# Row sums of every second transposed tile: folded on VectorE and multiplied once, instead of multiplied slice by slice

## The chip, the core and the metric

The kernel runs on one core of a Trainium2 chip. The core has TensorE (matrix products into PSUM banks of 128 x 512), VectorE and ScalarE (elementwise work and reductions), GpSimd and SyncE (here mostly queues that issue transfers), and 16 DMA engines that they share. Each engine runs its own instructions in program order and waits for the others by semaphores. The metric is device time in microseconds (us) for one execution.

## What is computed

Two layers of a graph network on 8192 nodes with 128 features. Cut to what matters:

```
adj_hat = adj + I
d = 1 / sqrt(sum(adj_hat, axis=1))
h = relu((adj_hat * d[:, None] * d[None, :]) @ (x @ W) + b)     # layer 0
x = layernorm(x + h)
s = x @ weight
o = relu(s + adj @ s + x @ self_weight)                           # layer 1
x = layernorm(x + pair_norm(o))
```

adj is 8192 x 8192 in f32, 268 MB, and is read about twice. The scale d needs the sum of each row of adj before any product of layer 0 with that row's z = d * (x W) can begin.

## The kernel before, in words

**Tiling.** adj is cut into 8 x 8 blocks of 1024 x 1024. A block comes as four chunks (q = 0..3) of 1 MB, each of two slices (JB = 2) of 128 x 1024. A chunk is loaded transposed (adjT) when it is multiplied and untransposed (adjN) when only its row sums are taken. Raw chunks go through a ring of buffers: four of their own (raw0 to raw3) and, for a time, parts of s1 and zr that are not in use yet (s34, s56, z67, z45, z23). SyncE's queue issues all these loads in one order; a load waits until the chunk that had its buffer is used up (`chunk.freed`).

**Products.** Matrix products are made in the rounded format f32r. ScalarE copies a slice rounded into hi (L514), VectorE subtracts to get the rest, lo (L687), and TensorE multiplies hi and lo with the rounded and hi with the rest of z: six products of 512 columns a slice (L982, L984, L988). hi and lo are rings of four slices (DEEP = 4): ScalarE may write slice n when TensorE has finished slice n - 4 (semaphore slice_multiplied), VectorE follows ScalarE (hi_ready), TensorE follows VectorE (slice_split).

**Stages.** Layer 0 starts before all row sums are known. In stage k (1 to 7) column k - 1 is multiplied: first its diagonal block (kept in o1, no load), then the blocks of rows k to 7, one after the other, four chunks each. The row sums of row i over columns left of the diagonal come from these same transposed slices: `add_sums` (L964) multiplies the slice's hi and lo with a pick matrix that has ones in one column, so that the sum lands in row i of the banks pC and pD: four more products a slice. The sums over columns right of the diagonal of row k are made from untransposed chunks that are loaded beside the products of stage k: on ScalarE as a copy with an accumulator (L520), for q = 3 on VectorE as a reduction (L693). The diagonal block of row k is loaded into o1 beside them ("keep"), and VectorE adds its eight slices into colsum by seven additions of 128 x 1024 (`sum_kept`, L703 and L707), each of which waits for the one before.

**The end of a stage.** After the eighth chunk from a stage's end (tail 0) TensorE runs `close_sums` (L998: two full-precision products of pick with colsum), ScalarE copies pC and pD (`read_sums`), TensorE turns them (`turn_degree`, L1008, tail 2), VectorE makes the degree (tail 4), TensorE `first_product` (L1018, tail 4), VectorE `make_z` (L736 to L741, tail 6). `add_visit_up` (L750) adds a finished row's products into ux, one chunk later. Which of these stand where is written by hand into the loops over the chunks, one loop an engine.

The table that follows the chunks sets which unit sums what (`Chunk.act`), whether a product chunk carries row sums (`Chunk.summed`), and when its buffer is free.

Of the kernel before, what the change touches and what calls it, by code (L numbers as in the profile page):

```python
# [8 lines left out]
class Chunk:  # L9
# [7 lines left out]
    cached: bool = False  # L17
    act: bool = False
    summed: bool = False
    stage: int = -1  # L20
    tail: int = -1
    buf: str = ""
# [29 lines left out]
def graph_kernel(nc, x, xT, adjT, adjN, W0, b_rows, W1, Wself, out):  # L52
    f32 = mybir.dt.float32
# [5 lines left out]
    P = 128  # L59
# [3 lines left out]
    BLK = 1024  # L63
    NB = N // BLK
    assert NB == 8
    Q = 4
    JB = 2
    TILE = JB * BLK
    HALF = 512
    H = 2  # L70
# [14 lines left out]
    def multiply_block(into, row, col, layers, visit, **more):  # L85
        for q in range(Q):
            into.append(Chunk("mul", row, col, q, layers=layers, visit=visit, **more))

    def new_visit(row, layers, phase, **more):
        visits.append(Visit(row, layers, phase, **more))  # L90
        return len(visits) - 1

    TAIL = 2 * Q
    products = []
    beside = defaultdict(list)
    for k in range(NB):
        sums = []
        for c in range(k + 1, NB):
            for q in range(Q):
                sums.append(Chunk("sum", k, c, q, act=(q % 2 == 0 if k == 0 else q != 3), stage=k))  # L100
        kept = [Chunk("keep", k, k, q, stage=k) for q in range(Q)]
        if k == 0:
            chunks += kept + sums
            continue
        first = len(products)
        multiply_block(products, k - 1, k - 1, (L0,), new_visit(k - 1, (L0,), 1, first=(k == 1)),
                       cached=True, stage=k)
        for i in range(k, NB):
            multiply_block(products, i, k - 1, (L0,), new_visit(i, (L0,), 1, first=(k == 1)),
                           summed=True, stage=k)  # L110
        for i, c in EXTRA.get(k, ()):
            multiply_block(products, i, c, (L0,), new_visit(i, (L0,), 1), stage=k)
        for n in range(first, len(products)):
            products[n].tail = n - (len(products) - TAIL)


        at = max(2 * Q, min(3 * Q, len(sums)))
        if k >= NB - 2:
            sums += [None] * (at - len(sums))
        sums[at:at] = kept  # L120
        room = [1.0] * Q + [0.5 if k < NB - 2 else 1.0] * Q + [1.0] * (len(products) - TAIL - first - Q)
        share, put = len(sums) / sum(room), 0
        if k >= NB - 2:
            share = 1.0
        for n in range(len(room)):
            upto = round(share * sum(room[:n + 1]))
            beside[first - Q + n] += [c for c in sums[put:upto] if c]
            put = max(put, upto)
        assert put >= len(sums)
# [39 lines left out]
    after_row0 = next(c for c in chunks if c.stage == 1)  # L169


    slices = act_sums = dve_sums = 0
    for chunk in chunks:
        if chunk.kind == "mul":
            chunk.base = slices
            slices += JB
            chunk.freed = ("split", slices)
            visits[chunk.visit].end = slices
        elif chunk.kind == "sum" and chunk.act:
            act_sums += 1  # L180
            chunk.freed = ("act", act_sums)
        elif chunk.kind == "sum":
            dve_sums += 1
            chunk.freed = ("dve", dve_sums)
# [106 lines left out]
    with ctx:  # L291
# [6 lines left out]
        def sem(name):  # L298
            return ctx.enter_context(nc.semaphore(name))
# [29 lines left out]

        xT_blk = s1[:, 0:BLK]  # L330
        colsum = s1[:, BLK:2 * BLK]
        rsum = [s1[:, 2 * BLK + r * NB * BG:2 * BLK + (r + 1) * NB * BG] for r in range(2)]
        kept = o1
        raw = {f"raw{r}": raw_own[r][:, :] for r in range(4)}
# [17 lines left out]
        sums = [pC, pD]  # L352
# [11 lines left out]
        act_summed = sem("act_summed")  # L364
        dve_summed = sem("dve_summed")
        col_step = sem("col_step")
        sums_closed = sem("sums_closed")
        sums_read = sem("sums_read")
        deg_turned = sem("deg_turned")
# [38 lines left out]
        dve_normed = sem("dve_normed")  # L408
        out_done = sem("out_done")

        raw_free = {"split": slice_split, "act": act_summed, "dve": dve_summed}
        bank_free = {"row": row_summed, "l0": l0_read, "dual": dual_read, "added": dual_added, "l1": l1_read,
                     "x1": x1_ready, "s1": s1_ready, "self": self_added}

# [14 lines left out]
        def slice_of(chunk, j):  # L429
            if chunk.kind == "keep" or chunk.cached:  # L430
                return kept[:, chunk.q * TILE + j * BLK:chunk.q * TILE + (j + 1) * BLK]
            return raw[chunk.buf][:, j * BLK:(j + 1) * BLK]
# [16 lines left out]
        @block.gpsimd  # L449
        def _(pool):  # L450
            pool.dma_start(w0[:, :], W0).then_inc(consts_in, 16)
            pool.dma_start(w1[:, :], W1).then_inc(consts_in, 16)
            pool.dma_start(t1[:, 0:P], Wself).then_inc(consts_in, 16)
            pool.dma_start(rows[:, :], b_rows).then_inc(consts_in, 16)
            pool.dma_start(xT_blk, xT[:, 0:BLK]).then_inc(xT_in, 16)
            pool.memset(ident[:, :], 0.0).then_inc(ident_zero, 1)
            pool.wait_ge(ident_zero, 1)
            pool.affine_select(out=ident[:, :], in_=ident[:, :], compare_op=ALU.not_equal, fill=1.0,
                               base=0, pattern=[[-1, P]], channel_multiplier=1).then_inc(ident_ready, 1)
            for k in range(1, NB):  # L460
                pool.wait_ge(y_done, k * H)
                pool.dma_start(xT_blk, xT[:, k * BLK:(k + 1) * BLK]).then_inc(xT_in, 16)
            pool.wait_ge(y_done, NB * H)
            pool.wait_ge(sums_closed, NB)
            for b in ("s34", "s56"):
                by, count = phase1_last[b]
                pool.wait_ge(raw_free[by], count)
            for k in FINAL_ROWS:
                pool.dma_start(groups(s1[:, k * BLK:(k + 1) * BLK]),
                               x[k * BLK:(k + 1) * BLK, :].rearrange("(g p) f -> p g f", p=P)).then_inc(x_in[k], 16)  # L470

            def store(k):
                pool.dma_start(out[k * BLK:(k + 1) * BLK, :].rearrange("(g p) f -> p g f", p=P),
                               groups(zr[:, k * BLK:(k + 1) * BLK])).then_inc(out_done, 16)

            def store_act(k):
                pool.wait_ge(act_normed, k + 1)
                store(k)

            def store_dve(i):  # L480
                pool.wait_ge(dve_normed, i + 1)
                store(i + NACT)

            for k in range(NACT - 1):
                store_act(k)
            for i in range(NB - NACT - 1):
                store_dve(i)
            store_act(NACT - 1)
            store_dve(NB - NACT - 1)
            pool.wait_ge(out_done, 16 * NB)  # L490
# [167 lines left out]
        def _(dve):  # L658
# [19 lines left out]
            def split_lo(chunk):  # L678
                for j in range(JB):
                    n = chunk.base + j  # L680
                    dve.wait_ge(hi_ready, n + 1)
                    if j == 0:
                        at = chunk.col * BLK + chunk.q * JB * P
                        for l, s, fresh in zip(chunk.layers, chunk.slots, chunk.fresh):
                            if fresh:
                                V.tensor_sub(rlo[s][:, :], (zr, s1)[l][:, at:at + JB * P], rhi[s][:, :].bitcast(f32))  # L686
                    V.tensor_sub(lo[n % DEEP][:, :], slice_of(chunk, j),  # L687
                                 hi[n % DEEP][:, :].bitcast(f32)).then_inc(slice_split, 1)

            def sum_rows(chunk):  # L690
                dve.wait_ge(*landed(chunk))
# [262 lines left out]
        def _(pe):  # L954
# [13 lines left out]
            def multiply(chunk):  # L968
                v = visits[chunk.visit]
                for j in range(JB):  # L970
# [20 lines left out]
                        last = add_sums(chunk, n)  # L991
                    last.then_inc(slice_multiplied, 1)

            def close_sums(k):
                pe.wait_ge(col_step, (k + 1) * (JB * Q - 1))
                to = pick[:, NB - 1 - k:NB - 1 - k + P].bitcast(f32)
                for h in range(H):
                    last = T.matmul(sums[h][:, :], to, colsum[:, h * HALF:(h + 1) * HALF],  # L998
                                    start=(k == 0), stop=True, skip_group_check=True)
                last.then_inc(sums_closed, 1)  # L1000
                closed[0] = k + 1
# [67 lines left out]
            first_product(0)  # L1069
            for n, chunk in enumerate(mul_chunks):  # L1070
                multiply(chunk)
                after_rows(n)
                if chunk.stage > 0 and chunk.tail == 0:
                    close_sums(chunk.stage)
                if chunk.stage > 0 and chunk.tail == 2:
                    turn_degree(chunk.stage)
                if chunk.stage > 0 and chunk.tail == 4:
                    first_product(chunk.stage)
# [45 lines left out]
```

## Time and profile before

| | us |
|---|---|
| median of three runs | 1904.98 (1902.94 to 1906.03) |
| the profiled execution | 1904.95, of which the span is 1903.1 |
| stage 2 (249.7 to 377.4) | 127.7 |
| stage 3 (377.4 to 486.3) | 108.9 |
| stage 4 (486.3 to 577.1) | 90.8 |
| stage 5 (577.1 to 653.0) | 75.9 |
| stage 6 (653.0 to 719.0) | 66.0 |
| stage 7 (719.0 to 775.7) | 56.7 |

A stage is taken from VectorE's split of its first slice to that of the next stage's. The rest of the span is stage 0 and 1 (to 249.7 us) and, after stage 7, the remaining blocks for both layers.

How to read the profile: PE is TensorE's matmuls, PEld its weight loads, DVE VectorE, ACT ScalarE, POOL GpSimd, SP SyncE's queue. L987 is line 987 of the program. A matmul's own length overlaps the next one's, so the time that one takes is read from start to start. Busy time is an average over a stretch, and says nothing of when within it. The granted clock (PEclk) is 1.00 at 2.4 GHz and 0.50 at 1.2 GHz.

### The profile page before, as it was taken

The page shows a single profiled execution, that of the slowest core. Times are in us where ns is not written, and L with a number is a line of the kernel's source. Part 1 is how long each engine was busy: PE and PEld are TensorE (multiplying, and loading weights), DVE is VectorE, ACT ScalarE, POOL GpSimd, SP SyncE. Part 2 cuts the span into 40 slices and gives each one's busy share as a digit, 9 for nine tenths or more (in the row PEclk, how much of TensorE's full clock was granted, in tenths as well). Part 3 has the DMA queues.
Part 4 walks back from the last instruction along what each step waited for, and adds up shares of the span by engine and source line. Part 5 has one row for each costly group of instructions (what it writes and reads, how often), then busy time and mean ns, then how long its engine had stood idle before and what let it go on. Part 6 is the DMA issues. An engine that isn't in the chain of part 4 may idle for free.

```text
span 1903.1 us, 20444 instructions
## 1 busy us (share of the span) xinstructions
PE 1732.4 (91%) x7682; PEld 1407.5 (74%) x7682; DVE 1454.5 (76%) x1898; ACT 1209.3 (64%) x1644; POOL 21.5 (1%) x34
## 2 busy tenths in 40 slices
PE   1099999999999999978999999999989999999983
PEld 0077778888887888767787788788868888877862
DVE  4486687686878679975777575575589999999987
ACT  3576686676856646654554554454468888888865
POOL 0000000000000000100000000000000000000001
PEclk7599999999999999999999999999999999999995
DMA  9999999999899568753444545545579999999943
GB/s 399 421 421 420 421 371 421 420 364 416 332 399 370 217 274 352 273 183 123 164 174 169 184 162 196 184 170 199 194 298 393 386 387 386 386 368 374 386 174 88
DMA packets 80291, 572.02 MB, mean 301 GB/s; under 512 B 8961, under 2 KB 8961, under 8 KB 12097
## 3 DMA queue, kind: packets, MB, share of 16 engines
q1 hardware_dynamic: 76608, 557.88, 74.9%
q0 software_dynamic: 3584, 12.85, 2.2%
q8 instruction: 60, 0.98, 0.2%
q14 instruction: 39, 0.31, 0.0%
HBM read 566.49 MB, written 4.19 MB: 300 GB/s over the span
## 4 chain that ended last, share of the span: by engine, by line
PE 75%; DVE 11%; DMA 9%; ACT 3%; issue 1%; SPq 0%; POOL 0%; ACTq 0%; DVEq 0%
PE acc L982 18%; PE acc L984 18%; PE acc L988 18%; DVE lo L687 6%; DMA s<-in_adjN 4%; PE pD L964 4%; PE pC L964 4%; DMA zr<-in_adjT 2%; DMA raw<-in_adjT 2%; ACT hi L514 1%; PE pA L982 1%; PE pA L984 1%; PE pA L988 1%; PE pB L982 1%; PE pB L988 1%
## 5 line engine op out<-in xcount | busy, mean ns | idle before, releaser
L982 PE MATMUL acc<-hi,rhi 128*128 128x512 f32 x1792 | 719.0, 401 | 44.3 <-DVE lo L687 26.5
L984 PE MATMUL acc<-lo,rhi 128*128 128x512 f32 x1792 | 702.1, 392 | 0.0
L687 DVE TENSOR_TENSOR lo<-raw,hi 128x1024 fp32r<-128x1024 f32 x528 | 627.4, 1220 | 77.1 <-ACT hi L514 73.1
L514 ACT ACTIVATE hi<-raw 128x1024 fp32r<-128x1024 f32 x528 | 544.3, 1055 | 168.5 <-PE pD L964 78.9
L988 PE MATMUL acc<-hi,rlo 128*128 128x512 f32 x1792 | 556.2, 392 | 0.0
L982 PEld LDWEIGHTS acc<-hi,rhi 128*128 128x128 f32 x1792 | 338.9, 189 | 135.3 <-DVE lo L687 42.6
L984 PEld LDWEIGHTS acc<-lo,rhi 128*128 128x128 f32 x1792 | 338.8, 189 | 73.1 <-issue 5.0
L988 PEld LDWEIGHTS acc<-hi,rlo 128*128 128x128 f32 x1792 | 338.5, 189 | 72.3
L687 DVE TENSOR_TENSOR lo<-zr,hi 128x1024 fp32r<-128x1024 f32 x188 | 225.3, 1222 | 43.6 <-ACT hi L514 40.7
L514 ACT ACTIVATE hi<-zr 128x1024 fp32r<-128x1024 f32 x188 | 197.2, 1059 | 53.5 <-PE acc L988 16.9
L686 DVE TENSOR_TENSOR rlo<-zr,rhi 128x256 fp32r<-128x256 f32 x123 | 52.1, 423 | 176.7 <-ACT hi L514 176.6
L508 ACT ACTIVATE rhi<-zr 128x256 fp32r<-128x256 f32 x123 | 50.8, 413 | 196.2 <-PE acc L988 196.2
L514 ACT ACTIVATE hi<-s 128x1024 fp32r<-128x1024 f32 x60 | 62.6, 1058 | 49.3 <-PE pD L964 36.4
L687 DVE TENSOR_TENSOR lo<-s,hi 128x1024 fp32r<-128x1024 f32 x60 | 71.8, 1222 | 27.9 <-ACT hi L514 27.5
L520 ACT ACTIVATE raw<-raw 128x1024 f32<-128x1024 f32 x66 | 68.9, 1045 | 31.3 <-DMA raw<-in_adjN 31.3
L964 PE MATMUL pC<-hi,pick 128*128 128x512 f32 x224 | 88.4, 394 | 0.0
L964 PE MATMUL pD<-hi,pick 128*128 128x512 f32 x224 | 88.1, 393 | 0.0
L964 PE MATMUL pD<-lo,pick 128*128 128x512 f32 x224 | 87.9, 393 | 0.0
L964 PE MATMUL pC<-lo,pick 128*128 128x512 f32 x224 | 87.8, 392 | 0.0
L514 ACT ACTIVATE hi<-o 128x1024 fp32r<-128x1024 f32 x64 | 66.5, 1055 | 16.9 <-PE pD L964 12.6
L687 DVE TENSOR_TENSOR lo<-o,hi 128x1024 fp32r<-128x1024 f32 x64 | 75.6, 1217 | 1.9 <-ACT hi L514 1.9
L686 DVE TENSOR_TENSOR rlo<-s,rhi 128x256 fp32r<-128x256 f32 x148 | 62.1, 420 | 7.7 <-ACT hi L514 7.1
(164 smaller groups left out, 1526.8 us busy)
## 6 DMA issues: line engine op xcount, KB each, us to landing
raw<-in_adjT SPq DMA_DIRECT2D x264, 1024.0 KB, 5.5
zr<-in_adjT SPq DMA_DIRECT2D x94, 1024.0 KB, 6.2
raw<-in_adjN SPq DMA_DIRECT2D x54, 1024.0 KB, 17.6
o<-in_adjT SPq DMA_DIRECT2D x32, 1024.0 KB, 10.5
s<-in_adjN SPq DMA_DIRECT2D x30, 1024.0 KB, 18.9
s<-in_adjT SPq DMA_DIRECT2D x30, 1024.0 KB, 14.7
zr<-in_adjN SPq DMA_DIRECT2D x28, 1024.0 KB, 19.5
s<-in_xT POOLq DMA_DIRECT2D x8, 512.0 KB, 8.0
```

Of the source, the lines that this page charges most:

```text
L508: S.activation(rhi[s][:, :], src[:, at:at + JB * P], ACT.Copy)
L514: S.activation(hi[n % DEEP][:, :], slice_of(chunk, j), ACT.Copy).then_inc(hi_ready, 1)
L520: ins = S.activation(slice_of(chunk, j), slice_of(chunk, j), ACT.Copy, accum_out=rsum[chunk.row % 2][:, g:g + 1])
L686: V.tensor_sub(rlo[s][:, :], (zr, s1)[l][:, at:at + JB * P], rhi[s][:, :].bitcast(f32))
L687: V.tensor_sub(lo[n % DEEP][:, :], slice_of(chunk, j), hi[n % DEEP][:, :].bitcast(f32)).then_inc(slice_split, 1)
L964: last = T.matmul(sums[h][:, :], to, mov[n % DEEP][:, h * HALF:(h + 1) * HALF], start=False, stop=False, skip_group_check=True)
L982: T.matmul(banks[h][:, :], a, hi[n % DEEP][:, part], start=opens, stop=False, skip_group_check=True)
L984: T.matmul(banks[h][:, :], a, lo[n % DEEP][:, part], start=False, stop=False, skip_group_check=True)
L988: last = T.matmul(banks[h][:, :], b, hi[n % DEEP][:, part], start=False, stop=end, skip_group_check=True)
```

## The change

From stage 2 on, every second block with row sums (row i in stage k where i - k is odd) carries them in another way. It is no longer `summed`: its slices get the six products only. VectorE adds its eight slices, in f32, into one slice `fold` (`fold_in`, seven additions of 128 x 1024, placed right behind the two splits of each chunk), and TensorE multiplies that slice once with the pick matrix in full precision (`add_fold`, two products of 512 columns), after the first chunk of the block that follows. Nine blocks are folded: rows 3, 5, 7 in stage 2; 4, 6 in stage 3; 5, 7 in stage 4; 6 in stage 5; 7 in stage 6. So 32 products of a block become two. An addition waits for the one before (fold_step); a block's first addition waits until the fold before has been multiplied (fold_summed); a folded chunk's raw buffer is free when its additions are done, not when it is split. The row-sum reductions of q = 3 go from VectorE to ScalarE for k > 1: 15 chunks.

```diff
-                sums.append(Chunk("sum", k, c, q, act=(q % 2 == 0 if k == 0 else q != 3), stage=k))
+                sums.append(Chunk("sum", k, c, q, act=(q % 2 == 0 if k == 0 else q != 3 or k > 1), stage=k))
...
         for i in range(k, NB):
+            fold = k > 1 and (i - k) % 2 == 1
             multiply_block(products, i, k - 1, (L0,), new_visit(i, (L0,), 1, first=(k == 1)),
-                           summed=True, stage=k)
+                           summed=not fold, folded=folds if fold else -1, stage=k)
+            folds += fold
...
+    FOLD = Q * JB - 1
+    def fold_steps(q):
+        return (q + 1) * JB - 1
...
-            chunk.freed = ("split", slices)
+            chunk.freed = ("split", slices) if chunk.folded < 0 else ("fold", FOLD * chunk.folded + fold_steps(chunk.q))
...
+        fold = s1[:, 7 * BLK:8 * BLK]
...
                     V.tensor_sub(lo[n % DEEP][:, :], slice_of(chunk, j),
                                  hi[n % DEEP][:, :].bitcast(f32)).then_inc(slice_split, 1)
+                if chunk.folded >= 0:
+                    fold_in(chunk)
+
+            def fold_in(chunk):
+                at = FOLD * chunk.folded + fold_steps(chunk.q) - JB
+                if chunk.q == 0:
+                    if chunk.folded > 0:
+                        dve.wait_ge(fold_summed, chunk.folded)
+                    V.tensor_add(fold, slice_of(chunk, 0), slice_of(chunk, 1)).then_inc(fold_step, 1)
+                    return
+                for j in range(JB):
+                    dve.wait_ge(fold_step, at + j)
+                    V.tensor_add(fold, fold, slice_of(chunk, j)).then_inc(fold_step, 1)
...
+            def add_fold(chunk):
+                pe.wait_ge(sums_read, closed[0])
+                pe.wait_ge(fold_step, FOLD * (chunk.folded + 1))
+                to = pick[:, NB - 1 - chunk.row:NB - 1 - chunk.row + P].bitcast(f32)
+                for h in range(H):
+                    last = T.matmul(sums[h][:, :], to, fold[:, h * HALF:(h + 1) * HALF],
+                                    start=False, stop=False, skip_group_check=True)
+                last.then_inc(fold_summed, 1)
...
                 multiply(chunk)
+                over = mul_chunks[n - 1]
+                if n > 0 and over.folded >= 0 and over.q == Q - 1:
+                    add_fold(over)
```

VectorE in row 4 of stage 3, before: lo is the split, ux the addition of row 3's products, `s<-o` and `s<-s,o` are colsum.

```order
L687 TENSOR_TENSOR lo<-raw,hi 128x1024 x4
L693 TENSOR_REDUCE s<-raw 128x2
L687 TENSOR_TENSOR lo<-s,hi 128x1024 x2
L750 TENSOR_TENSOR ux<-ux,acc 128x512 x2
L703 TENSOR_TENSOR s<-o 128x1024
L687 TENSOR_TENSOR lo<-s,hi 128x1024 x2
L707 TENSOR_TENSOR s<-s,o 128x1024 x2
L687 TENSOR_TENSOR lo<-zr,hi 128x1024 x2
L707 TENSOR_TENSOR s<-s,o 128x1024 x4
L687 TENSOR_TENSOR lo<-zr,hi 128x1024 x2
```

The same place now (L702 is the split, L713 and L717 the fold, L779 ux, L732 and L736 colsum):

```order
L702 TENSOR_TENSOR lo<-raw,hi 128x1024 x4
L713 TENSOR_TENSOR s<-raw 128x1024
L702 TENSOR_TENSOR lo<-s,hi 128x1024 x2
L717 TENSOR_TENSOR s<-s 128x1024 x2
L779 TENSOR_TENSOR ux<-ux,acc 128x512 x2
L732 TENSOR_TENSOR s<-o 128x1024
L702 TENSOR_TENSOR lo<-s,hi 128x1024 x2
L717 TENSOR_TENSOR s<-s 128x1024 x2
L736 TENSOR_TENSOR s<-s,o 128x1024 x2
L702 TENSOR_TENSOR lo<-zr,hi 128x1024 x2
L717 TENSOR_TENSOR s<-s,zr 128x1024 x2
L736 TENSOR_TENSOR s<-s,o 128x1024 x4
```

Between the splits of this block stood seven colsum additions and one reduction; now there are seven more additions and no reduction.

TensorE in the second slice of row 5 of stage 3, now (L1011, L1013, L1017 are the six products of a slice, L1029 the fold's):

```order
L1011 MATMUL acc<-hi,rhi 128x512
L1013 MATMUL acc<-lo,rhi 128x512
L1011 MATMUL acc<-hi,rhi 128x512
L1013 MATMUL acc<-lo,rhi 128x512
L1017 MATMUL acc<-hi,rlo 128x512 x2
L993 MATMUL pC<-hi,pick 128x512
L993 MATMUL pC<-lo,pick 128x512
L993 MATMUL pD<-hi,pick 128x512
L993 MATMUL pD<-lo,pick 128x512
L1029 MATMUL pC<-s,pick 128x512
L1029 MATMUL pD<-s,pick 128x512
```

The slices of the folded block no longer have the L993 group; the pair L1029 stands behind the first chunk of the next block.

## Rows read from the trace of the kernel before

**Rows 1.** The page: each engine's busy time, share of the span, instructions

```profile
PE 1732.4 (91%) x7682; PEld 1407.5 (74%) x7682; DVE 1454.5 (76%) x1898; ACT 1209.3 (64%) x1644; POOL 21.5 (1%) x34
```

**Rows 2.** Busy time by stretch, stages 2, 3 and 4

```profile
core 0: us, PE busy (x) PEld busy (x) DVE busy (x) ACT busy (x) POOL busy (x), PEclk, DMA share, GB/s
...
249.70:377.40 127.70, 126.63 (x565) 103.13 (x564) 97.28 (x96) 91.14 (x124) 0.53 (x1) 1.00 0.98 402
377.40:486.30 108.90, 108.19 (x485) 88.17 (x484) 84.72 (x85) 78.59 (x108) 0.53 (x1) 1.00 0.95 386
486.30:577.10 90.80, 90.05 (x405) 73.18 (x404) 71.52 (x75) 61.82 (x84) 0.53 (x1) 1.00 0.94 369
```

**Rows 3.** Waits, 249.7 to 719 us: total, times, longest

```profile
PE acc L982 <- DVE lo L687: 6.0, 7, 1.7
...
ACT hi L514 <- PE pD L964: 121.5, 111, 3.3
```

**Rows 4.** TensorE in order of time: start, length; a summed and an unsummed slice

```profile
402.84 0.39 PE L982 MATMUL acc<-hi,rhi 128*128 128x512 f32 x1
...
405.11 0.39 PE L982 MATMUL acc<-hi,rhi 128*128 128x512 f32 x1
...
381.51 0.39 PE L982 MATMUL acc<-hi,rhi 128*128 128x512 f32 x1
...
382.87 0.39 PE L982 MATMUL acc<-hi,rhi 128*128 128x512 f32 x1
```

**Rows 5.** TensorE in order of time: close_sums of stage 2

```profile
344.12 1.02 PE L998 MATMUL pC<-s,pick 128*128 128x512 f32 x2
344.98 1.02 PE L998 MATMUL pD<-s,pick 128*128 128x512 f32 x2
```

**Rows 6.** VectorE in order of time, row 4 of stage 3

```profile
414.35 1.28 DVE L750 TENSOR_TENSOR ux<-ux,acc 128x512 f32<-128x512 f32 x2
415.55 1.22 DVE L703 TENSOR_TENSOR s<-o 128x1024 f32<-128x1024 f32 x1
416.68 2.35 DVE L687 TENSOR_TENSOR lo<-s,hi 128x1024 fp32r<-128x1024 f32 x2
418.95 2.48 DVE L707 TENSOR_TENSOR s<-s,o 128x1024 f32<-128x1024 f32 x2
421.35 2.35 DVE L687 TENSOR_TENSOR lo<-zr,hi 128x1024 fp32r<-128x1024 f32 x2
```

**Rows 7.** Busy time by stretch: single blocks of the stages, columns as in rows 2

```profile
284.90:303.00 18.10, 18.10 (x81) 15.01 (x80) 17.96 (x18) 8.51 (x8) 0.00 (x0) 1.00 1.02 423
361.60:381.50 19.90, 19.90 (x97) 16.75 (x96) 14.41 (x19) 15.14 (x23) 0.53 (x1) 1.00 1.01 419
411.90:430.00 18.10, 18.10 (x81) 14.95 (x80) 17.89 (x18) 10.47 (x12) 0.00 (x0) 1.00 1.01 425
448.40:470.50 22.10, 22.10 (x102) 17.51 (x101) 11.33 (x13) 11.65 (x14) 0.00 (x0) 1.00 1.01 420
...
594.60:637.10 42.50, 40.77 (x181) 32.25 (x180) 33.13 (x32) 20.14 (x22) 0.00 (x0) 1.00 0.78 302
686.50:708.20 21.70, 21.70 (x101) 17.42 (x100) 12.22 (x14) 9.57 (x10) 0.00 (x0) 1.00 0.51 203
```

**Rows 8.** Groups by line and shape: busy, mean ns, idle before

```profile
L693 DVE TENSOR_REDUCE s<-raw 128x2 f32<-128x2048 f32 x21 | 47.9, 2280 | 17.4 <-DMA raw<-in_adjN 17.4
```

**Rows 9.** VectorE in order of time: make_z of stage 2, first and last

```profile
368.54 0.20 DVE L736 RECIPROCAL d<-sq 128x8 f32<-128x8 f32 x1
...
370.19 0.68 DVE L741 TENSOR_TENSOR zr<-pB,d 128x512 f32<-128x512 f32 x1
```

**Rows 10.** Busy time by stretch: where TensorE stood, and a low clock

```profile
179.30:181.90 2.60, 0.01 (x1) 0.01 (x1) 1.29 (x2) 2.00 (x2) 0.00 (x0) 1.00 1.01 419
182.90:186.30 3.40, 3.40 (x9) 2.66 (x8) 0.79 (x2) 3.11 (x6) 0.00 (x0) 0.51 1.01 419
...
855.40:865.60 10.20, 5.28 (x13) 4.15 (x14) 5.56 (x16) 2.04 (x4) 0.00 (x0) 0.50 0.29 104
```

More of the change, by code:

```diff
@@ L19 @@
     summed: bool = False
+    folded: int = -1
     stage: int = -1
@@ L93, in graph_kernel @@
     TAIL = 2 * Q
+    folds = 0
     products = []
@@ L366, in graph_kernel @@
         col_step = sem("col_step")
+        fold_step = sem("fold_step")
+        fold_summed = sem("fold_summed")
         sums_closed = sem("sums_closed")
@@ L409, in graph_kernel @@
         out_done = sem("out_done")
-        raw_free = {"split": slice_split, "act": act_summed, "dve": dve_summed}
+        raw_free = {"split": slice_split, "act": act_summed, "dve": dve_summed, "fold": fold_step}
         bank_free = {"row": row_summed, "l0": l0_read, "dual": dual_read, "added": dual_added, "l1": l1_read,
@@ L467, in _ @@
                 pool.wait_ge(raw_free[by], count)
+            pool.wait_ge(fold_summed, folds)
             for k in FINAL_ROWS:
```

## The prediction

> **What bounds the kernel now.** I read the page first, then stretches by stage, the waits, and instructions in order of time. TensorE is busy 91% of the span, VectorE 76% [rows 1]. The change touches only stages 2 to 6, and there TensorE has 126.6 of 127.7 us, 108.2 of 108.9 and 90.0 of 90.8 [rows 2]. Between 249.7 and 719 us it waits 6.0 us in total, while ScalarE waits 121.5 us for TensorE to give back a split buffer [rows 3]. So TensorE sets the pace and the two splitting engines stand behind it, at most four slices ahead (DEEP). The reader should then see how near the next two limits are. The transfers move 402, 386 and 369 GB/s in stages 2 to 4 [rows 2] against about 420 when they don't stop [rows 7]. And VectorE's average of 76% hides blocks in which it has nothing left: from 284.9 to 303.0 us it is busy 17.96 of 18.10 us, from 411.9 to 430.0 us 17.89 of 18.10 [rows 7]. These are blocks beside which the diagonal's own tiles are added into colsum (seven adds in a stage), and stages 2 to 4 each fold just such a block: row 3 in stage 2, row 4 in stage 3, row 5 in stage 4.
>
> **What TensorE sheds and gains.** A slice with row sums takes 405.11 - 402.84 = 2.27 us, one without 382.87 - 381.51 = 1.36 us [rows 4]: the four products cost 0.91. A folded block has eight slices, so 7.3 us go. It gets two full-precision products on the folded slice. Their like in close_sums start 0.86 us apart [rows 5], so a pair is 1.72 us. Nine blocks are folded (three in stage 2, two in stages 3 and 4 each, one in 5 and 6 each): 65.7 us go, 15.5 come, 50 net. That is TensorE's work and not yet time.
>
> **What VectorE gets.** Seven adds of 128x1024 per folded block, each waiting for the one before. The nearest rows are the same operation on colsum. A pair of splits takes 418.95 - 416.68 = 2.27 us; a pair of adds 421.35 - 418.95 = 2.40 [rows 6]. A folded chunk (two splits, two adds) is 4.67 us of VectorE, against 2.72 of TensorE without the sums and 4.54 before with them. In return 15 reductions of 2.28 us [rows 8] move to ScalarE; ScalarE has 91.1 of 127.7 us in stage 2 [rows 2], so it carries them, at up to 0.7 us of delay in a folded block. Before, these reductions mostly lay in VectorE's waits, so moving them gains where VectorE led, only stage 5 (below).
>
> On the adds: the waiting pair takes 0.13 us longer start to start than the pair of splits with no wait [rows 6]. By "VectorE: DVE Perf Modes" of the Trainium skill, section "The DRAIN you can't avoid", a semaphore after each operation costs nothing extra; the adds would then run at 2.27 a pair and 27 pairs would take 3.5 us less than I count. The row decides for 2.40.
>
> **A folded block without colsum adds.** ScalarE may write a slice only once TensorE has released the one four back, so VectorE's split of the second chunk begins about when TensorE finishes the block before. From there to the first slice of the next block VectorE has three chunks (3 x 4.67), the addition of the ended block into ux (1.20, a pair in [rows 6]) and one split (1.13): 16.4 us. TensorE took 18.1 before. The gain on the block is 1.8, not 7.3, and the two products (after the next block's first chunk, queued ahead of its second on TensorE, with VectorE's lead then at nothing) take back 1.72. In the middle of a stage a fold is worth nothing.
>
> **The blocks one by one**, from the start of their first product to that of the next block's:
> - Row 3, stage 2: five colsum adds fall inside (6.0 us), and ScalarE is 0.7 late: 16.4 + 6.0 + 0.7 = 23.0 against 18.1, +4.9.
> - Row 4, stage 3, and row 5, stage 4: all seven inside (8.4): 24.8 against 18.1, +6.7 each.
> - Row 5, stage 2: 16.4 against 18.2, -1.8.
> - Row 6, stage 3: close_sums and turn_degree lie in the block, 22.1 us before [rows 7]; they now hide in TensorE's idle time: 16.4, -5.7.
> - Rows 5 and 6, stage 5: 42.5 before [rows 7], in which VectorE was behind already (TensorE 40.8 busy). Without the reduction of 2.28 row 5 takes 18.2. Row 6 then starts without a lead: 16.4 plus one split and one add, 18.6. Together 36.8, -5.7.
> - Row 7, stage 6: 21.7 before [rows 7], 18.6 after, -3.1.
> - Row 7, stages 2 and 4: VectorE also has make_z there (2.3, from 368.54 to the end at 370.87) [rows 9] and small steps that I put at 0.8: 19.5 against 19.9 [rows 7], -0.4 each.
> - The products: 9 x 1.72 = 15.5, of which 1.8 lies in waits of the cached blocks behind the two rows 7: +13.7.
>
> The sum is 4.9 + 13.4 - 1.8 - 5.7 - 5.7 - 3.1 - 0.8 + 13.7 = **+14.9 us**. Freeing a raw buffer only after the fold costs nothing: transfers of stage 3 have slack once the engines are later than they are.
>
> **The clock.** After TensorE stood still for 2.6 us at 179.3, the granted clock was 0.51 (the lower level, 1.2 GHz) from 182.9 to 186.3 us; from 855.4 it stayed at 0.50 for 10.2 us [rows 10]. In the three blocks with colsum adds a chunk takes VectorE 7.1 us and TensorE 2.7, so it stands for some 4 us at a time. While it waits a lower clock costs nothing; the next block starts at it. Bounds: none, and 10.2 us at half rate each (5.1 x 3 = 15.3). I take the row at 182.9, 3.4 us at half rate: 1.7 x 3 = **5.1**. Everything after stage 6 only moves. The profiled execution took 1904.95 us (span 1903.1), which is the runs' median of 1904.98. Forecast: 1904.95 + 14.9 + 5.1 = **1925.0 us**.
>
> **Rivals.**
> A, TensorE stays the bound. VectorE's 97.3 busy us of 127.7 [rows 2] have room for stage 2's 14.2 more (21 adds less five reductions). Then 5.6 us a block go, until the transfers bind: 127.7 x (1 - 402/420) = 5.5 in stage 2, 8.8 in stage 3, 11.0 in stage 4, and 5.6 each in stages 5 and 6: 36.5 us, **1868.5**. Against it: the room lies at the wrong place [rows 7] and four slices can't carry it there. [...]
> B, the colsum adds are absorbed: VectorE keeps a lead big enough that blocks with them cost what the others do. It decides if the folded blocks at rows 3, 4 and 5 take 16.4: 14.9 - 4.9 - 13.4 - 5.4 = -8.8 and no clock loss, **1896**. Absorbed by half, about +3, **1908**, no measurable change. For it: the adds wait for nothing but their tiles, and those are loaded early. Against: VectorE runs strictly in program order and the adds stand between the splits.
> C, the low clock spreads: the other six folded blocks leave gaps of about 2 us in each 4.7, and at the lower clock a chunk without sums takes 5.4 us, longer than VectorE's 4.67. With 5.3 busy us at half rate (2.65 lost, as at 855.4) behind each of nine blocks: 14.9 + 23.9, **1944**. By "TensorE: Matmul & The Clock Gate", section "HAM oscillation — how this bites in real kernels", of the Trainium skill, a loop that waits between bursts starts each burst at the low clock; the stretches at 182.9 and 855.4 agree, each behind a wait [rows 10].
>
> **Numbers.** Forecast with its milder forms (1909 to 1937) 0.60, C 0.17, A 0.05, B in full 0.08, B by half 0.10. The likeliest case's own range is 1909 to 1937, from the clock's bounds and a microsecond either way in the three long blocks. The range that should hold the time 8 times in 10 leaves out A, B in full and the end of C: 1904 to 1944. About 0.2% is what a measurement can tell from no change. Faster 0.13, same 0.10, slower 0.77.
>
> **What would show it.** Right: TensorE waits for VectorE's lo or fold for 60 us or more in stages 2 to 6; stages 3 and 4 longer than before and stage 5 shorter; the folded block of stage 3 near 25 us; VectorE in the chain. Wrong: stage 2 near 121 us with transfers at 420 GB/s (A); folded blocks with colsum adds near 18 us (B); a low clock across whole blocks outside the three (C).

## The result, and the profile after

The change makes the kernel slower: 1923.89 us median of four runs (1921.76 to 1924.33) against 1904.72 (1902.94 to 1906.03), a ratio of 1.0101 with a 95% interval of 1.0085 to 1.0116. The forecast was 1925.0. The profiled execution took 1921.76 us, span 1920.0.

The page after the change: span, then each engine's busy time, share and instructions.

```profile
span 1920.0 us, 20057 instructions
...
PE 1703.6 (89%) x7430; PEld 1370.4 (71%) x7430; DVE 1492.3 (78%) x1946; ACT 1237.9 (64%) x1704; POOL 21.4 (1%) x34
```

TensorE has 28.8 us less to do than in [rows 1], and the span is 16.9 us longer. (Busy time counts time at the lower clock in full, so the work that went is more than 28.8.)

The busy time by stretch, stages 2 to 6 of the changed kernel, columns as in [rows 2]: engines' busy us, granted clock, share of the transfer engines, GB/s.

```profile
249.90:387.70 137.80, 119.18 (x493) 92.78 (x492) 110.35 (x112) 103.64 (x150) 0.53 (x1) 0.95 0.92 374
387.70:503.70 116.00, 102.65 (x428) 79.83 (x427) 91.77 (x96) 83.61 (x118) 0.53 (x1) 0.94 0.91 368
503.70:604.00 100.30, 86.52 (x351) 67.51 (x350) 80.94 (x86) 68.58 (x98) 0.53 (x1) 0.91 0.82 329
604.00:674.50 70.50, 66.22 (x288) 51.34 (x287) 61.91 (x69) 48.08 (x66) 0.53 (x1) 0.99 0.76 305
674.50:738.10 63.60, 60.73 (x273) 48.49 (x272) 61.52 (x69) 36.40 (x40) 0.53 (x1) 1.00 0.69 273
```

Stages 2, 3 and 4 grew by 10.1, 7.1 and 9.5 us, stages 5 and 6 shrank by 5.4 and 2.4: +18.9. In the first three TensorE is busy 308.3 of 354.1 us where before it had 324.9 of 327.4 [rows 2]. The transfers ran at 374, 368 and 329 GB/s, less than before, and ScalarE waited 14.6 us for them in stages 2 to 6 where it had waited 23.1. After stage 7 some 2 us of it are given back: between 795 and 885 us the granted clock falls three times in the trace of before (at 800.7, 828.0 and 855.4) and twice in that of after (at 821.0 and 872.2), and such a fall costs about 1.7 (below).

What TensorE waits for, 249.7 to 740 us, to be held against [rows 3]: total, times, longest.

```profile
PE acc L1011 <- DVE lo L702: 52.8, 25, 6.6
...
ACT hi L529 <- PE pD L993: 74.9, 52, 7.6
```

6.0 us have become 52.8, all of it for VectorE's splits. ScalarE's wait for the last product of a slice with row sums (pD) fell from 121.5 to 74.9, but a folded slice ends with another product (acc), and the wait for that one rose from 5.9 to 43.0: together 127.4 us became 117.9. VectorE's share of the chain that ends last rose from 11% to 19%.

The block on which the forecast rested, row 4 of stage 3. First VectorE in order of time (start, length): L702 is the split, L717 the fold, L779 the addition of row 3's products, L732 and L736 colsum.

```profile
422.86 2.48 DVE L717 TENSOR_TENSOR s<-s 128x1024 f32<-128x1024 f32 x2
425.26 1.28 DVE L779 TENSOR_TENSOR ux<-ux,acc 128x512 f32<-128x512 f32 x2
426.45 1.22 DVE L732 TENSOR_TENSOR s<-o 128x1024 f32<-128x1024 f32 x1
427.59 2.35 DVE L702 TENSOR_TENSOR lo<-s,hi 128x1024 fp32r<-128x1024 f32 x2
429.86 2.48 DVE L717 TENSOR_TENSOR s<-s 128x1024 f32<-128x1024 f32 x2
432.25 2.48 DVE L736 TENSOR_TENSOR s<-s,o 128x1024 f32<-128x1024 f32 x2
434.65 2.35 DVE L702 TENSOR_TENSOR lo<-zr,hi 128x1024 fp32r<-128x1024 f32 x2
436.92 2.48 DVE L717 TENSOR_TENSOR s<-s,zr 128x1024 f32<-128x1024 f32 x2
439.31 5.06 DVE L736 TENSOR_TENSOR s<-s,o 128x1024 f32<-128x1024 f32 x4
444.30 2.35 DVE L702 TENSOR_TENSOR lo<-zr,hi 128x1024 fp32r<-128x1024 f32 x2
```

No row has an idle time behind it: VectorE works without a break from 422.86 until it reaches the next block's first split at 444.30, and a chunk's splits come 7.06 us apart (427.59, 434.65) while TensorE needs 2.7 for a chunk. Then the busy time of this block, the block behind it, and of the three stretches of low clock.

```profile
420.20:445.60 25.40, 14.18 (x50) 10.33 (x49) 24.71 (x23) 13.94 (x18) 0.00 (x0) 0.79 1.01 423
445.60:467.20 21.60, 21.60 (x84) 16.92 (x85) 13.92 (x13) 11.47 (x15) 0.00 (x0) 0.93 0.98 404
...
308.80:312.20 3.40, 3.40 (x10) 2.66 (x9) 3.37 (x4) 0.91 (x3) 0.00 (x0) 0.50 1.01 419
441.90:448.70 6.80, 3.13 (x7) 2.48 (x8) 6.77 (x6) 0.21 (x2) 0.00 (x0) 0.50 0.93 361
561.30:564.80 3.50, 3.50 (x11) 2.69 (x10) 3.50 (x5) 0.12 (x1) 0.00 (x0) 0.51 1.00 412
```

The block took 25.4 us where it had 18.1 [rows 7]; VectorE is busy for 24.7 of them, TensorE for 14.2. Behind it the clock is at its lower level when TensorE starts on the next block's full work, each time for 3.1 to 3.5 busy us.

### The profile page after: what moved, and what is told of

The parts are those of the page before. It is cut to its first block, busy times and chain, and to the rows that moved or that the text cites. A ratio compares the mean times of both kernels' runs of the same rounds, so it can differ in the third digit from the quotient of the medians.

```text
span 1920.0 us, 20057 instructions
## 1 busy us (share of the span) xinstructions
PE 1703.6 (89%) x7430; PEld 1370.4 (71%) x7430; DVE 1492.3 (78%) x1946; ACT 1237.9 (64%) x1704; POOL 21.4 (1%) x34
## 4 chain that ended last, share of the span: by engine, by line
PE 62%; DVE 19%; DMA 9%; ACT 6%; issue 3%; SPq 0%; POOL 0%; ACTq 0%; DVEq 0%
PE acc L1011 16%; PE acc L1013 16%; PE acc L1017 15%; DVE lo L702 9%; DMA s<-in_adjN 4%; ACT hi L529 3%; DMA zr<-in_adjT 2%; DVE s L717 2%; DMA raw<-in_adjT 2%; PE pC L993 2%; PE pD L993 2%; DVE s L736 2%; ACT s L535 1%; DVE ux L779 1%; ACT raw L535 1%
## 5 line engine op out<-in xcount | busy, mean ns | idle before, releaser
L1011 PE MATMUL acc<-hi,rhi 128*128 128x512 f32 x1792 | 728.8, 407 | 90.5 <-DVE lo L702 73.0
L1013 PE MATMUL acc<-lo,rhi 128*128 128x512 f32 x1792 | 707.7, 395 | 0.0
L702 DVE TENSOR_TENSOR lo<-raw,hi 128x1024 fp32r<-128x1024 f32 x528 | 626.5, 1220 | 66.0 <-ACT hi L529 62.1
L1017 PE MATMUL acc<-hi,rlo 128*128 128x512 f32 x1792 | 560.4, 394 | 0.0
L1011 PEld LDWEIGHTS acc<-hi,rhi 128*128 128x128 f32 x1792 | 341.5, 191 | 191.6 <-DVE lo L702 98.7
L1013 PEld LDWEIGHTS acc<-lo,rhi 128*128 128x128 f32 x1792 | 342.0, 191 | 74.0 <-issue 6.0
L1017 PEld LDWEIGHTS acc<-hi,rlo 128*128 128x128 f32 x1792 | 341.8, 191 | 73.9
L702 DVE TENSOR_TENSOR lo<-zr,hi 128x1024 fp32r<-128x1024 f32 x188 | 224.7, 1221 | 43.4 <-ACT hi L529 40.7
L535 ACT ACTIVATE raw<-raw 128x1024 f32<-128x1024 f32 x88 | 91.8, 1045 | 31.0 <-DMA raw<-in_adjN 31.0
L529 ACT ACTIVATE hi<-s 128x1024 fp32r<-128x1024 f32 x60 | 62.5, 1056 | 47.0 <-PE pD L993 22.6
L702 DVE TENSOR_TENSOR lo<-s,hi 128x1024 fp32r<-128x1024 f32 x60 | 71.4, 1220 | 19.4 <-ACT hi L529 19.2
L702 DVE TENSOR_TENSOR lo<-o,hi 128x1024 fp32r<-128x1024 f32 x64 | 75.3, 1217 | 0.6 <-ACT hi L529 0.6
L1057 PE MATMUL pA<-w,s 128*128 128x128 f32 x64 | 9.4, 295 | 58.9 <-DVE deg L755 58.9
L535 ACT ACTIVATE s<-s 128x1024 f32<-128x1024 f32 x52 | 54.3, 1046 | 11.1 <-DMA s<-in_adjN 11.0
L523 ACT ACTIVATE rhi<-s 128x256 fp32r<-128x256 f32 x148 | 59.5, 402 | 2.8 <-PE acc L1017 2.8
L993 PE MATMUL pC<-hi,pick 128*128 128x512 f32 x152 | 60.7, 399 | 0.0
## 6 DMA issues: line engine op xcount, KB each, us to landing
s<-in_adjN SPq DMA_DIRECT2D x30, 1024.0 KB, 18.9
```

The costliest lines, as they stand in the source:

```text
L523: S.activation(rhi[s][:, :], src[:, at:at + JB * P], ACT.Copy)
L529: S.activation(hi[n % DEEP][:, :], slice_of(chunk, j), ACT.Copy).then_inc(hi_ready, 1)
L535: ins = S.activation(slice_of(chunk, j), slice_of(chunk, j), ACT.Copy, accum_out=rsum[chunk.row % 2][:, g:g + 1])
L702: V.tensor_sub(lo[n % DEEP][:, :], slice_of(chunk, j), hi[n % DEEP][:, :].bitcast(f32)).then_inc(slice_split, 1)
L993: last = T.matmul(sums[h][:, :], to, mov[n % DEEP][:, h * HALF:(h + 1) * HALF], start=False, stop=False, skip_group_check=True)
L1011: T.matmul(banks[h][:, :], a, hi[n % DEEP][:, part], start=opens, stop=False, skip_group_check=True)
```

## Experiments

Lengths of blocks below are from the start of TensorE's first product of a block to that of the next.

### The two halves of the change, alone

TensorE's half. The fold's additions on VectorE are left out; `fold` is set to zero once, and the pair multiplies that.

```diff
-            chunk.freed = ("split", slices) if chunk.folded < 0 else ("fold", FOLD * chunk.folded + fold_steps(chunk.q))
+            chunk.freed = ("split", slices)
...
+            V.memset(fold, 0.0).then_inc(fold_step, 1)
...
-                if chunk.folded >= 0:
-                    fold_in(chunk)
...
-                pe.wait_ge(fold_step, FOLD * (chunk.folded + 1))
+                pe.wait_ge(fold_step, 1)
```

> TensorE's part of the change alone: the folded blocks have no row-sum products and the pair behind them multiplies a slice of zeros; VectorE's additions into fold are left out, so part of the row sums is missing. Theory (VectorE's program order sets the folded blocks): without the adds a folded block needs 3 x 2.27 + 1.2 + 1.13 = 9.1 us of VectorE, plus 8.4 (6.0 in stage 2) where colsum adds lie inside, so those three blocks still take 15 to 18 us and the others fall to 11; transfers cap stage 2 at -5.5. Sum -5.5 - 4.5 - 4.5 - 7.8 - 5.6 = -28: 1877 us. Rival A (TensorE the bound everywhere, transfers the cap): 1868 us, and all nine blocks near 11 us. If it stays above 1900, neither: then the loss was not in the adds.

Measured: 1885.7 us, one execution. Its busy time by stretch: row 4 of stage 3, row 6 of stage 3, row 5 of stage 2, and a stretch of low clock across the end of row 4 of stage 3.

```profile
410.30:428.40 18.10, 11.65 (x49) 8.66 (x47) 17.57 (x17) 11.09 (x14) 0.00 (x0) 0.96 1.01 423
451.00:465.50 14.50, 14.50 (x69) 11.55 (x69) 10.21 (x12) 11.65 (x14) 0.00 (x0) 1.00 1.01 423
320.30:339.40 19.10, 13.53 (x49) 9.73 (x47) 9.86 (x11) 16.16 (x24) 0.00 (x0) 0.91 1.02 422
...
427.00:433.80 6.80, 5.38 (x13) 4.26 (x14) 5.97 (x7) 4.84 (x7) 0.00 (x0) 0.51 1.02 422
```

This half does bring time, 19 us, but not where VectorE is full. In row 4 of stage 3 TensorE has 11.7 us of work and the block still takes 18.1, since VectorE is busy for 17.6 of them without any fold: that block had nothing to give from the start. The three blocks with colsum adds took 15.4, 18.1 and 16.8 us, as said. Row 6 took 14.5, since close_sums and turn_degree still lie in it (22.1 - 7.3 = 14.8; the 11 that I had written for such blocks forgot them). Row 5 of stage 2 took 19.1 with neither engine full, at 422 GB/s: there the transfers bind, and ScalarE waits for each tile to land. Rival A's 36.5 us are not there even with VectorE's half left out. The expected 28 was too much by 9, and 5 of the 9 lie in stage 3: row 6 kept its 3.5 us, and the block behind row 4 began at the lower clock, which the expectation had left out; it took 22.6 us, 2.5 more than before with the pair. The rest is spread over stages 2, 4 and 5 (1.6, 1.2 and 1.0).

VectorE's half. All slices keep their row-sum products, the fold is added up and never multiplied.

```diff
-                           summed=not fold, folded=folds if fold else -1, stage=k)
+                           summed=True, folded=folds if fold else -1, stage=k)
...
-                if n > 0 and over.folded >= 0 and over.q == Q - 1:
-                    add_fold(over)
```

> VectorE's part alone: the nine blocks keep their 32 row-sum products, the additions into fold are made but never multiplied, the reductions of q = 3 are on ScalarE. Theory: the three blocks with colsum adds take 23.0, 24.8 and 24.8 us as in the change (+18.3), the others stay at TensorE's 18.2 or 22.1, row 5 of stage 5 gains 2.2: about 1921 us. The block behind each of the three takes 18.2 to 18.6, since TensorE has no pair there, and if it stands less, no low clock: in the change those took 21.6. Rival A: the adds hide in VectorE's idle time, 1905 us or less. Rival on the clock (the 1.7 us behind those blocks come from VectorE being late, not from the clock): those blocks take about 20 us here too.

Measured: 1923.1 us, one execution, as slow as the whole change. The busy time by stretch of rows 4 and 5 of stage 3, rows 5 and 6 of stage 4, and of the low clock in stage 3.

```profile
416.50:441.90 25.40, 20.29 (x82) 15.95 (x81) 24.73 (x23) 14.06 (x18) 0.00 (x0) 0.93 1.01 423
441.90:461.90 20.00, 20.00 (x80) 16.21 (x81) 13.89 (x13) 11.36 (x15) 0.00 (x0) 0.91 1.00 411
534.30:558.80 24.50, 20.70 (x81) 15.81 (x79) 24.30 (x23) 9.37 (x10) 0.00 (x0) 0.93 1.01 422
558.80:581.00 22.20, 22.16 (x100) 17.60 (x101) 14.18 (x15) 11.14 (x14) 0.00 (x0) 1.00 0.73 272
443.10:446.50 3.40, 3.40 (x9) 2.63 (x8) 3.29 (x4) 0.90 (x1) 0.00 (x0) 0.51 0.92 349
```

The long blocks are 25.4 and 24.5 us, to a tenth what they are in the change, though TensorE is busy in them for 6.1 and 5.4 us more than in the change. So their length is VectorE's. The six other folded blocks kept their length of before to 0.1 us. The blocks behind the three show the clock apart from the pair: without pairs they took 18.4, 20.1 and 22.2 us, 0.3, 1.7 and 0.1 more than before, and only the middle one began at the lower clock. In the change the same blocks took 3.5, 3.3 and 3.4 more, 1.72 of it for the pair. The fall behind a block in which TensorE keeps standing thus costs about 1.7 us. With TensorE busier in the long blocks it hit one block behind them and not three; that is one execution.

### Only the reductions moved

```diff
-            fold = k > 1 and (i - k) % 2 == 1
+            fold = False
```

> Only the 15 reductions of q = 3 go from VectorE to ScalarE; nothing is folded. Theory: they lay in VectorE's waits except in row 5 of stage 5, which falls from 20.4 to about 18.2: 1903 us. Rival (ScalarE has no room for them and starts its splits late): blocks of stage 2 to 4 with sums beside them grow by 0.7 or more each, 1908 us or above.

Measured: 1904.94 us, one execution. All blocks of stages 2 to 6 kept their length to 0.1 us but row 5 of stage 5, which fell from 20.4 to 19.3: half of what the theory said, and the rival's growth is absent. Where stage 7 ends the kernel is 1.1 us ahead; the total doesn't show it, since the low clock that lies at 828.0 us before, for 3.4 us, lies here at 825.2 for 6.8.

VectorE's splits of the second chunk of that block, in the kernel before and then with the reductions moved:

```profile
597.18 1.21 DVE L687 TENSOR_TENSOR lo<-raw,hi 128x1024 fp32r<-128x1024 f32 x1
...
596.08 2.36 DVE L701 TENSOR_TENSOR lo<-raw,hi 128x1024 fp32r<-128x1024 f32 x2 [0.91 <-ACT hi L528]
```

VectorE is rid of 2.2 us and starts only 1.1 earlier, for it now waits for ScalarE, which takes the same reduction (592.92 to 595.0 us) ahead of the copy that VectorE needs. In the other blocks ScalarE carries the reductions at no cost.

### Without the three folds beside colsum adds

```diff
-            fold = k > 1 and (i - k) % 2 == 1
+            fold = k > 1 and (i - k) % 2 == 1 and (k, i) not in ((2, 3), (3, 4), (4, 5))
```

> The change without the three folds that lie beside colsum adds (row 3 of stage 2, row 4 of stage 3, row 5 of stage 4); six folds stay. Theory: -1.8 - 5.7 - 5.7 - 3.1 - 0.8, and six pairs of 1.72 of which 1.8 hide, +8.5: -8.6, no low clock, 1896 us. Rival A: six blocks by 5.6 with the transfers' cap in stage 2, -28: 1877 us. If the three blocks are not the cause, it stays near 1917 us (two thirds of the loss).

Measured: 1895.50 us median of four, ratio 0.9950 (0.9933 to 0.9966). Three of nine folds carry more than the whole loss; the other six together gain 9.5 us. Row 5 of stage 5 again took longer than forecast (19.4 us instead of 18.2). One more block came out otherwise: row 5 of stage 2 took 18.5 us (16.4 expected, 16.6 in the change). The busy time of that block in this kernel, and two of ScalarE's rows and one of VectorE's in order of time, just ahead of its start at 321.3 and behind it:

```profile
321.30:339.80 18.50, 13.32 (x50) 9.61 (x48) 16.91 (x17) 15.43 (x23) 0.00 (x0) 0.91 1.02 422
...
319.75 1.06 ACT L535 ACTIVATE s<-s 128x1024 f32<-128x1024 f32 x1 [0.48 <-DMA s<-in_adjN]
322.24 2.01 ACT L529 ACTIVATE hi<-s 128x1024 fp32r<-128x1024 f32 x2 [0.30 <-DMA s<-in_adjT]
...
323.33 2.36 DVE L702 TENSOR_TENSOR lo<-s,hi 128x1024 fp32r<-128x1024 f32 x2 [1.48 <-ACT hi L529]
```

ScalarE takes each tile as it lands, so VectorE enters the block with no lead over TensorE: it splits the second chunk 2 us behind the block's start, where the sum of 16.4 has that split begin with the block. From there to the next block it works without a break and needs the 16.4. In the change this block came 8 us later, the transfers were ahead, and it took 16.6.

### Folds only where TensorE has the most and VectorE the least

```diff
-            fold = k > 1 and (i - k) % 2 == 1
+            fold = i == NB - 2 and k < 6 or (k, i) == (6, 7)
```

> Six folds, and only in the blocks in which TensorE also has close_sums and turn_degree and no colsum adds lie: row 6 of stages 1 to 5, row 7 of stage 6. Theory: each of the first five goes from 22.1 to 16.4 us (-5.7), row 7 of stage 6 from 21.7 to 18.6 (-3.1), and six pairs of 1.72 come: -28.5 - 3.1 + 10.3 = -21, 1884 us. Rival A: 6 x 5.6 = 33.6 less, 1871 us. Rival (transfers bind behind a shorter block): 1895 us, with the gain of a block given back in the next one.

Measured: 1890.21 us median of four, ratio 0.9922 (0.9905 to 0.9938): between the theory and its rival. The blocks took 18.6, 18.6, 16.8, 17.7, 18.5 and 17.9 us and the block behind each grew by 1.9 us, hardly more than the pair: nothing else was given back. The busy time by stretch of row 6 in stages 2 and 3, and VectorE's splits of the second chunk of each:

```profile
338.00:356.60 18.60, 15.21 (x70) 11.48 (x69) 18.50 (x18) 13.55 (x16) 0.00 (x0) 1.00 1.01 422
445.40:462.10 16.70, 15.06 (x69) 11.33 (x67) 16.60 (x17) 12.71 (x15) 0.00 (x0) 1.00 1.01 421
...
340.11 2.35 DVE L702 TENSOR_TENSOR lo<-s,hi 128x1024 fp32r<-128x1024 f32 x2
445.69 2.35 DVE L702 TENSOR_TENSOR lo<-raw,hi 128x1024 fp32r<-128x1024 f32 x2
```

VectorE is full in both, 18.50 of 18.60 and 16.60 of 16.70; the difference is how much of the first chunk's work lies inside the block: the second chunk's splits begin 2.1 us behind the start of the first block and 0.3 us behind that of the second. So a block that starts without a lead costs 18.6, not 16.4. To tell this from the transfers, the first chunk was left out of the fold:

```diff
...
+            fold_from = 1 if i == NB - 2 and k < 6 or (k, i) == (6, 7) else Q
+            for chunk in products[whole + fold_from:]:
+                chunk.summed, chunk.folded, chunk.begins = False, folds, chunk.q == fold_from
...
```

> As e2_before_last_row, but the first chunk of each of the six blocks keeps its row-sum products and only the other three are folded (five additions). Theory: VectorE needs 16.2 us from the block's first split to the next block's even without a lead, TensorE 22.1 - 6 x 0.91 = 16.6: all six blocks at 16.3 to 16.6 instead of 18.6, 18.6, 16.8, 17.7, 18.5 and 17.9, -9 in sum: 1881 us. Rival (the missing 2 us in e2_before_last_row are the transfers', not VectorE's lead): no change or a little worse, 1890 us or above.

Measured: 1881.45 us median of four, ratio 0.9875 (0.9860 to 0.9890). All six blocks took 16.3 to 16.5 us. The busy time by stretch of row 6 in stages 2 and 5:

```profile
336.00:352.50 16.50, 16.50 (x77) 13.06 (x77) 16.31 (x16) 12.61 (x15) 0.00 (x0) 1.00 1.02 423
598.60:615.10 16.50, 16.50 (x78) 13.15 (x78) 16.43 (x16) 11.66 (x14) 0.00 (x0) 1.00 0.54 192
```

Row 6 of stage 2 gained 2.1 us though its transfers ran at 423 GB/s as before, so the 2 us were VectorE's. Now TensorE and VectorE are both full. Folding less brought more, and this version beats both kernels.

A step further, three additions in six more blocks:

```diff
+            fold_from = 1 if i == NB - 2 and k < 6 or (k, i) == (6, 7) else 2 if (k, i) in ((2, 5), (2, 7), (3, 5), (3, 7), (4, 7), (5, 7)) else Q
```

> As e8_three_of_four, and in six more blocks without colsum adds (rows 5 and 7 of stages 2 and 3, row 7 of stages 4 and 5) the last two chunks are folded (three additions, 16 products become two). Theory: each gives 8 us slices at 0.91 for four slices, 3.65, less the pair at 1.85: -1.8 each where VectorE has its 3.6 us free and the transfers don't bind (not in row 5 of stage 2): -9: 1872 us. Rival (VectorE's lead is gone by then and the additions show): 1881 us or above.

Measured: 1883.46 us median of four, ratio 0.9885 (0.9868 to 0.9902): the rival's time, and no gain over three chunks of four in six blocks, but another mechanism than the rival's shows. VectorE's wait in this kernel, 330 to 357 us:

```profile
DVE s L714 <- PE pD L1030: 4.6, 1, 4.6
```

There is one `fold` slice. When two blocks in a row are folded, VectorE's first addition waits until TensorE has multiplied the fold before, and its splits stand behind that addition. Rows 6 of stages 2 and 3 took 21.2 and 19.6 us instead of 16.5 and 16.4. A second `fold` slice would take this wait away; no run has one.

### All nine folds, but the colsum adds a block earlier

```diff
-        at = max(2 * Q, min(3 * Q, len(sums)))
+        at = 2 * Q
```

> All nine folds as in the change, but the diagonal's tiles are loaded and added into colsum four chunks earlier, so that in stages 2 to 4 most colsum adds lie in the block ahead of the folded one. Theory (what made the three blocks long is that both kinds of adds met in one block): row 4 of stage 3 and row 5 of stage 4 go from 25 us to 18.8 (or 21 if VectorE starts them without a lead), row 3 of stage 2 from 22.6 to 19 to 21; the low clock behind them goes. 1903 to 1910 us. Rival (the nine folds are too much for VectorE wherever the colsum adds lie): what the folded blocks give back appears in the blocks ahead of them, 1918 us or more.

Measured: 1907.27 us median of ten, ratio 1.0010 (1.0000 to 1.0020), as expected, and no gain over the kernel before. The busy time by stretch of row 4 in stage 3, with row 3 ahead of it:

```profile
398.00:416.50 18.50, 18.50 (x82) 15.14 (x82) 16.82 (x17) 11.12 (x13) 0.00 (x0) 1.00 1.02 423
...
416.50:437.10 20.60, 13.55 (x50) 9.61 (x48) 20.46 (x20) 18.75 (x29) 0.00 (x0) 0.92 0.91 361
```

The folded block fell from 25.4 to 20.6 us between the 18.8 expected with a lead and the 21 without one, its neighbour took in most of the colsum adds at no cost (18.3 us from start to start, as before), and no low clock lay behind it. It is the meeting of the two chains of additions in one block that costs, not their number.

### The additions on GpSimd

```diff
...
+                for j in range(JB):
+                    pool.wait_ge(fold_step, at + j)
+                    nc.gpsimd.tensor_add(fold, fold, slice_of(chunk, j)).then_inc(fold_step, 1)
...
```

> The change with the 63 additions into fold on GpSimd instead of VectorE (a raw buffer is then free when both its split and its addition are done). Theory: VectorE's program order was the cost, so the blocks fall to what e4_products_alone shows, as long as GpSimd's seven additions end before the next block's first chunk does (under 2.3 us each): near 1877 us. An estimate from the Trainium skill, GPSIMD Engine Reference, section Performance versus the Vector engine (4.5 us at 2048 columns, so about 2.25 at 1024): 15.8 us a block, just enough. Rival (the additions disturb VectorE or come late): TensorE waits for the fold, or VectorE's splits get longer than 1.22 us, 1900 us or above.

Measured: 1951.50 us median of four, ratio 1.0247 (1.0232 to 1.0262): wrong by 75 us. VectorE in order of time in row 5 of stage 5, ahead of and in the time of GpSimd's additions for row 6, and the busy time of that stretch.

```profile
629.33 2.35 DVE L722 TENSOR_TENSOR lo<-raw,hi 128x1024 fp32r<-128x1024 f32 x2
631.61 6.73 DVE L748 TENSOR_TENSOR s<-s,o 128x1024 f32<-128x1024 f32 x2
638.26 6.66 DVE L722 TENSOR_TENSOR lo<-raw,hi 128x1024 fp32r<-128x1024 f32 x2
...
631.20:653.70 22.50, 11.24 (x39) 8.41 (x37) 22.43 (x8) 4.24 (x4) 21.84 (x7) 0.83 0.58 236
```

A pair of splits that takes 2.35 us takes 6.66 while GpSimd adds. In 22.5 us VectorE gets 8 operations done and GpSimd 7. This block, not folded itself, took 34.1 us.

## Why the prediction was right

**The bound.** That VectorE's program order sets a folded block held: VectorE's half of the change alone gives its whole loss (1923.1 us against 1923.9), and the long blocks are the same to 0.1 us with and without the products.

**Term by term**, forecast and then measured, in us against before. Rows 3, 4 and 5 of stages 2, 3 and 4, with colsum adds: +4.9, +6.7, +6.7; +4.4, +7.2, +6.2. Row 5 of stage 2: -1.8; -1.7. Row 6 of stage 3: -5.7; -5.4. Rows 5 and 6 of stage 5: -5.7; -4.8. Row 7 of stage 6: -3.1; -3.9. The rows 7 of stages 2 and 4: -0.4 each; -0.8 and -0.5. Pairs and clock together, read in the nine blocks behind: +18.8; +18.6. Measured, they sum to 19.3 against the forecast's 20.0, and stage 7's first block gives back 0.4, which leaves the 18.9 of the stages above. The profiled execution ends 16.9 behind that of before, since it has one fall of the clock less after stage 7; the medians are 19.2 apart.

**The step that was too big** is the reduction that leaves row 5 of stage 5. I took off all of its 2.28 us; only 1.2 came, in the change and with the reductions alone, since ScalarE does the reduction just ahead of the slice for which VectorE then waits.

**The pair** starts at 488.52 and 489.38 and the next product at 490.24, 1.72 us as from [rows 5].

```profile
488.52 1.02 PE L1029 MATMUL pC<-s,pick 128*128 128x512 f32 x2
489.38 1.02 PE L1029 MATMUL pD<-s,pick 128*128 128x512 f32 x2
490.24 1.05 PE L1057 MATMUL pA<-w,s 128*128 128x128 f32 x8
```

**The clock** cost 1.8, 1.5 and 1.7 us behind the three blocks, where the forecast took 1.7 from the row at 182.9, and not more: rival C's spread to the other six blocks is absent. In the kernel without the three folds the clock fell inside folded blocks (its granted mean is 0.91 in the row of 321.3 above), but behind none of them did a block grow by more than 1.9 us, the pair and 0.2.

**The semaphore.** "The DRAIN you can't avoid" in "VectorE: DVE Perf Modes" of the Trainium skill says that a wait after each operation costs nothing extra. In the rows of the block above a pair of fold additions takes 2.39 us (429.86 to 432.25), a pair of splits 2.27 (427.59 to 429.86): the measured 0.12 decides, as the forecast had it. The page measured copies; no run here has the same additions without the wait, so that the 0.12 is the wait's is not shown.

**What the forecast took for granted** and what held only by luck: a lead of VectorE's at the start of a folded block. In the change it was there: row 5 of stage 2 came 8 us later than in the kernel without the three folds, and ScalarE did not wait for a tile in it. Where the change is cut down it is not, and the block costs 2 us more (18.5 and 18.6 against 16.4 to 16.8). This is why the expectation for folds in row 6 alone was 6 us too low.

**What was off.** The forecast's own sign, that TensorE waits 60 us or more for VectorE, was missed: it waits 52.8. The range of the likeliest case, 1909 to 1937, does not follow from what it is said to come from: without any clock loss and with 3 us less in the three long blocks the sum is 1917, and with all of it 1938. The time lies in both. And the terms given for a folded block without colsum adds sum to 16.3, not 16.4; it took 16.6 in row 5 of stage 2 and row 6 of stage 3.

**The rivals.** A fell twice: the kernel became slower, and with VectorE's half left out it gains 19 us and not 36.5. B's mechanism exists, as the run with the colsum adds a block earlier shows: the block ahead takes them in for nothing. But it is not there in the order in which the change has them.

## What to carry to other kernels

Before work is moved from the busiest engine to one with idle time, read the receiving engine's busy time in the very stretch where the work will stand, not over the stage: 76% on average was 99% in three blocks (two in [rows 7], the third below, from before), and those three turned a gain of 9 us into a loss of 19. A ring of four slices can't carry idle time from one block into another. Move only as much as makes both engines end together: three chunks of four in the right six blocks gave 1.2%, all four gave 0.8%, every second block cost 1.0%.

```profile
520.80:539.10 18.30, 18.30 (x81) 14.99 (x80) 18.20 (x18) 8.01 (x8) 0.00 (x0) 1.00 1.01 422
```

## What the runs showed of the hardware

GpSimd and VectorE hold each other up when both add tiles from SBUF. Alone, VectorE's operation on 128x1024 starts every 1.13 to 1.25 us; with GpSimd adding, one of each finished every 3.3 us (pairs of 6.66 and 6.73 above), and GpSimd's addition took 3.12 us on average. "SBUF — State Buffer" in the Trainium skill, section "SBUF: two separate sides", describes it: the port pair that both use is an exclusive lock, held for the whole instruction, against a VectorE operation with two SBUF inputs when GpSimd reads SBUF too. The trace agrees in its numbers, since one operation of each finishes per 3.3 us, though its rows overlap and don't show the turns themselves. I had counted on 2.25 us for GpSimd's addition, an estimate from the figure for 2048 columns in "GPSIMD Engine Reference" of the Trainium skill, section "Performance versus the Vector engine" (4.5 us), and not on the turns; no run shows GpSimd adding alone.

```profile
L480 POOL TENSOR_TENSOR s<-s,raw 128x1024 f32<-128x1024 f32 x30 | 93.7, 3124 | 18.8 <-DMA raw<-in_adjT 15.9
```

That row is GpSimd's group of additions in that kernel: busy, mean ns, idle before.
